# Splitting the first two experts' weights on GpSimd in the front of an attention and mixture-of-experts kernel

## The reference

```python
xn = _layernorm(x)
out = x + attention(xn) + ffn(xn)

# attention: 16 heads of 8, causal mask
q, k, v = split(xn @ in_proj.T)
p = softmax(q @ k.T / sqrt(8) + mask)
attention = (p @ v) @ out_proj.T

# ffn: one shared expert and 7 routed ones, the best 2 for each token
expert(h, g, u, d) = (silu(h @ g.T) * (h @ u.T)) @ d.T      # 128 -> 352 -> 128
probs = softmax(xn @ wr.T + rb); the two largest, scaled to sum 1
ffn = shared(xn) + sum over the two chosen experts of weight * expert(xn)
```

## Time and profile before

| what | us |
|---|---|
| time, median of 3 runs without a profile | 467.42 (467.25 to 471.32) |
| the profiled execution (its span, the one time that its page has) | 485.8 |
| TensorE busy in the profiled execution | 439.9 (91%) |
| GpSimd busy | 302.7 (62%) |
| granted TensorE clock, mean | 0.987 |

### The profile page before, as it was taken

One profiled execution on the slowest core, in us unless ns is written; L12 is line 12 of the kernel. 1 busy time (PEld: TensorE's weight loads), 2 busy tenths in 40 slices (PEclk: granted clock), 3 DMA queues, 4 the chain that ended last, 5 costly groups with the idle time before them and its releaser, 6 DMA issues.

```text
span 485.8 us, 12527 instructions
## 1 busy us (share of the span) xinstructions
PE 439.9 (91%) x3983; PEld 329.3 (68%) x3987; DVE 359.8 (74%) x804; ACT 312.8 (64%) x709; POOL 302.7 (62%) x439
## 2 busy tenths in 40 slices
PE   8888897988998989999889999998999899979995
PEld 4666565665666666666555688786877788868884
DVE  6885997987878877778774387585765777566987
ACT  2756676775867677767677676565565766555552
POOL 1326887997887888887888500755547487845300
PEclk9999999998999999999999999999999999989998
DMA  8776798999875555666356337787777767821762
GB/s 233 229 240 233 230 329 294 295 332 331 266 232 153 156 164 174 173 177 168 119 165 255 90 84 214 242 290 225 225 234 247 239 195 258 299 60 35 245 204 65
DMA packets 60415, 102.00 MB, mean 210 GB/s; under 512 B 11045, under 2 KB 29226, under 8 KB 59328
## 3 DMA queue, kind: packets, MB, share of 16 engines
q1 hardware_dynamic: 55872, 92.74, 61.2%
q0 software_dynamic: 4480, 8.47, 5.2%
HBM read 62.49 MB, written 39.46 MB: 210 GB/s over the span
## 4 chain that ended last, share of the span: by engine, by line
PE 62%; ACT 7%; POOL 6%; issue 5%; DVE 4%; SPq 4%; DMA 2%; another core or an unknown queue 2%; DVEq 0%; ACTq 0%; POOLq 0%
PE ps L850 11%; PE ps L848 11%; PE ps L849 11%; PE ps L917 6%; PE ps L978 6%; PE ps L925 4%; ACT sb_work L706 4%; POOL sb_work L620 3%; POOL xs L596 2%; PE ps L998 2%; DMA sb_ring<-qk 2%; PE ps L1143 2%; PE ps L981 2%; SPq L471 2%
## 5 line engine op out<-in xcount | busy, mean ns | idle before, releaser
L1343 DVE TENSOR_REDUCE sb_blockmax<-ps 128x6 f32<-128x768 f32 x128 | 121.5, 956 | 37.2 <-PE ps L925 32.4
L706 ACT ACTIVATE sb_work<-ps 128x768 f32<-128x768 f32 x128 | 104.7, 818 | 64.7 <-PE ps L913 63.5
L648 POOL DMA_INDIRECT ys<-sb_v_all,sb_xn_all x76 | 81.3, 1069 | 72.3 <-DVE sb_v_all L1464 52.6
L620 POOL TENSOR_SCALAR_AFFINE_SELECT sb_work<-sb_work 128x512 f32<-128x512 f32 x128 | 82.2, 646 | 27.6 <-ACT sb_work L706 25.5
L849 PE MATMUL ps<-sb_ring,sb_wb 128*128 128x512 f32 (+1 forms) x231 | 83.6, 362 | 0.0
L1443 DVE TENSOR_TENSOR sb_v_all<-ps,sb_v_all 128x512 f32<-128x512 f32 (+1 forms) x93 | 57.5, 618 | 24.4 <-ACT sb_v_all L796 10.6
L596 POOL DMA_INDIRECT xs<-sb_xn_all,sb_posu x64 | 62.9, 983 | 10.6 <-issue 10.6
L917 PE MATMUL ps<-sb_ring 32*128 32x256 f32 x256 | 49.5, 377 | 20.7 <-ACT sb_work L706 10.1
L796 ACT ACTIVATE sb_v_all<-ps 128x512 f32<-128x512 f32 (+1 forms) x93 | 49.7, 534 | 10.5 <-PE ps L850 5.4
L917 PEld LDWEIGHTS ps<-sb_ring 32*128 32x128 f32 x256 | 25.6, 183 | 44.9 <-issue 38.4
L848 PE MATMUL ps<-sb_ring,sb_wb 128*128 128x512 f32 (+1 forms) x138 | 51.6, 374 | 3.3 <-issue 1.8
(11 more groups left out here) (168 smaller groups left out, 1089.0 us busy)
## 6 DMA issues: line engine op xcount, KB each, us to landing
sb_wb<-wd SPq DMA_DIRECT2D x75, 384.0 KB
sb_ring<-qk SPq DMA_DIRECT2D x64, 256.0 KB
wd<-sb_wb SPq DMA_DIRECT2D x8, 1152.0 KB, 5.9
xs<-sb_o_all SPq DMA_DIRECT2D x19, 260.0 KB, 4.2
qk<-sb_ring SPq DMA_DIRECT2D x32, 128.0 KB
sb_work<-ys SPq DMA_DIRECT2D x16, 256.0 KB, 3.2
sb_xn_all<-xs SPq DMA_DIRECT2D x15, 260.0 KB
sb_o_all<-w SPq DMA_DIRECT2D x8, 384.0 KB, 3.9
```

The costliest lines, as they stand in the source:

```text
L620: pool.affine_select(out=o, in_=o, compare_op=ALU.is_ge, fill=0.0, base=0, pattern=[[0, 4], [1, 128]], channel_multiplier=-1)\
L648: pool.indirect_dma_start(out=ys_d, out_offset=bass.IndirectOffsetOnAxis(ap=row, axis=0), in_=yst[i % NYS][:, EMB * j:EMB * j + EMB], in_o ...
L706: act.activation(part.rearrange("p (k h q) -> p h k q", h=2, q=128), ps[:, 4:6, 0:HEAD].rearrange("p h (k q) -> p h k q", q=128), ACT.Exp, ...
L1343: dve.tensor_reduce(blockmax[:, a:b + 1, 0:3], ps[:, a:b + 1, 0:HEAD].rearrange("p h (k c) -> p h k c", c=128), AX.X, ALU.max).then_inc(s[ ...
```

## The change

A constant `AHEAD = 2` says how many experts are split in the front.

- GpSimd: in the front's loop over its six norm pairs, each pair is followed by one block: expert 0's three blocks behind `f = 5, 7, 9`, expert 1's behind `f = 11, 13, 15`. The memsets of `v_sb` and `ones_b`, which stood ahead of `split_block` in the file, now follow that loop. In the steps, the block at `n` is that of the expert two further on, and the last is at `n = 16` in place of 22.
- SP: the loads of experts 0 and 1 move from `n = -4` and `n = -1` to the place ahead of the constant tile's four DMAs. At `n = -4` and `n = -1` SP now loads experts 2 and 3, which wait for the splits of 0 and 1, and stores 0 and 1. The later loads stand at `n = 2, 5, 8, 11`, the stores at `n = 2, 5, ..., 17`.
- TensorE, VectorE and ScalarE have the same instructions in the same order.

```diff
+AHEAD = 2
...
+            for e in range(AHEAD):
+                load_expert(e)
             sp.wait_ge(s["kzero"], 1)
             sp.wait_ge(s["kone"], 1)
             for b in range(4):
...
-                if (n + 4) % 3 == 0 and 0 <= (n + 4) // 3 < EXPERTS:
-                    load_expert((n + 4) // 3)
-                if (n - 2) % 3 == 0 and 0 <= (n - 2) // 3 < EXPERTS:
-                    store_expert((n - 2) // 3)
+                if (n + 4) % 3 == 0 and AHEAD <= (n + 4) // 3 + AHEAD < EXPERTS:
+                    load_expert((n + 4) // 3 + AHEAD)
+                if (n - 2) % 3 == 0 and 0 <= (n - 2) // 3 + AHEAD < EXPERTS:
+                    store_expert((n - 2) // 3 + AHEAD)
...
-            for f in range(5, NB, 2):
+            for i, f in enumerate(range(5, NB, 2)):
                 pool.wait_ge(s["rs"], f // 2 + 1)
                 for t in (2 * f, 2 * f + 1):
                     last = pool.tensor_scalar(...)
                 last.then_inc(s["xp"], 1)
+                split_block(i // MT, i % MT)
...
-                if 0 <= n + 1 < MT * EXPERTS:
-                    split_block((n + 1) // MT, (n + 1) % MT)
+                if 0 <= n + 1 < MT * (EXPERTS - AHEAD):
+                    split_block((n + 1) // MT + AHEAD, (n + 1) % MT)
```

More of the change, by code:

```diff
@@ L593, in split_block @@
                 pool.wait_ge(s["wsp"], e + 1)
+            for i, f in enumerate(range(5, NB, 2)):
+                pool.wait_ge(s["rs"], f // 2 + 1)
+                for t in (2 * f, 2 * f + 1):
+                    last = pool.tensor_scalar(xn_all[:, t, 0:EMB], x_sb[:, t, :], mv[:, t, 0:1], rstd[:, t:t + 1],
+                                              ALU.subtract, ALU.mult)
+                last.then_inc(s["xp"], 1)
+                split_block(i // MT, i % MT)
+            for k, buf in enumerate(v_sb):
+                pool.memset(buf, 0.0).then_inc(s["vz"], 1)
+                pool.wait_ge(s["vz"], k + 1)
+                pool.memset(buf[:, :, :, HD:HD + 1], 1.0).then_inc(s["v1"], 1)
+            pool.memset(ones_b[:, :], 1.0).then_inc(s["onesb"], 1)
             def send(k, t):
```

## The result

The changed kernel took 476.91 us (median of 4 runs, 471.80 to 479.24) against 467.34 us before (466.43 to 471.32). The ratio is 1.0162, 95% interval 1.0111 to 1.0214: 1.6% slower, outside the range of 463.0 to 471.8. An execution over 1.5% above the shortest of its kernel (here that of 479.24) counts as slow and is in no ratio, so a ratio can differ from the quotient of the medians (here 1.0205). The profiled execution is one of 478.70 us, with a span of 477.0.

The account below looks back on a forecast made before the run. TensorE was taken as busy for 91% of the span, with VectorE pacing 27 to 39 us of the front. The terms +1.9 + 0 + 1.0 - 2.3 - 0.6 came to 0.0 us: 467.5 us, range 463.0 to 471.8.

Parts of the forecast that it names:

- The loads ahead of the constant tile: Front: ten DMAs on SP delay writes and first read-back, so the front ends 1.9 us later (0.6 to 3.5).
- The blocks behind the norms: Front: GpSimd's split blocks fit its gaps, hidden behind VectorE's statistics, at no cost; about 1 us if expert 0 loads late.
- SP behind GpSimd: Steps 3 to 9: SP's queue waits for GpSimd's blocks, +1.0 us (0 to 2.9); as slower rival 472.6 us, chance 0.18.
- The later experts sooner: Steps 17 to 25: without those loads, splits and stores, 2.3 plus 0.6 us gained, 2.9 together (0 to 5.5).
- The rivals: DMA relief 462.5 us (0.18), SP's queue 472.6 (0.18), VectorE's routing pacing steps 17 to 22 469.7 (0.09), port lock 469.6 (0.05).
- The ports: Front rival: VectorE's five shifts each wait for a GpSimd subtraction on shared ports, +2.2 us, 469.6 us, chance 0.05.

Follow-up runs that it names:

- before_again: The kernel before, unchanged, run for a second profiled execution: 467.76 us, with a span of 466.0 us.
- third_buffer: The changed kernel with a buffer of its own for sequence 2's query and key pair: 474.87 us, ratio 1.0153 to the kernel before.
- fill: The changed kernel with 22 unused matmuls on constant data in TensorE's two waits: 472.08 us, ratio 1.0094 to the kernel before.
- one_ahead: The changed kernel with expert 1's load moved behind the first three read-backs: 469.24 us, ratio 1.0044 to the kernel before.
- pool_loads: The changed kernel with the first two experts' ten load DMAs on GpSimd's queue, before its first norms: 468.07 us, ratio 1.0030.
- tile_first: The changed kernel with only expert 0's load early, behind the constant tile, and four zero fills moved to later steps: 469.44 us, ratio 1.0042.

## Why the prediction was wrong

The profiled executions of before_again and of the changed kernel give the account: front +11.6 us, steps 0 to 2 -0.4, steps 3 to 8 +0.9, steps 9 to 16 +0.1, steps 17 to 25 -1.2. That is +11.0, and the spans differ by 11.0 (477.0 less 466.0); the medians, by 9.6. The forecast had +1.9, 0, +1.0, 0 and -2.9. No term of the forecast had the -0.4: in steps 0 to 2 the kernel before has a granted clock of 0.84 and the changed one 1.00, as their windows show; why was not found.

- *The loads ahead of the constant tile: +1.9, wrong.* This is the step that failed. Its rows were right at first: the constant tile was forecast at 14.95 and went at 15.02; sequence 0's writes at 17.5 and went at 17.65. Two things were missing behind that. The writes were followed only to the read-back, and not to the buffer that they free: `qk_h[0]`, for which ScalarE waited 1.95 us and TensorE 2.70 in place of 0.89. And "the front ends 1.9 us later" took every later instruction at its old duration. With waits of 2 to 3 us in it TensorE fell to 1.2 GHz and became the bound in VectorE's place. third_buffer shows that taking the first wait away is not enough, fill that the clock is some 8 of the 11.6 us. The read-back itself was also later than forecast (25.27, not 23.85), because SP was held up inside the writes (2.08 us for two; the upper bound of 3.5 had allowed for such a hold-up), and step -3 began at 29.00, not 27.3.
- *The blocks behind the norms: 0, right.* In one_ahead they are all there and step 0 begins at 44.24 us against 44.11.
- *SP behind GpSimd: +1.0, right by number, not by reason.* 22.93 less 22.03 is 0.9. But that holds for a front 11.6 us late; with the front in time steps 3 to 8 lose 3.6 us (one_ahead) or 3.3 (pool_loads), above the upper bound of 2.9, which was worked out for just that case, and steps 3 to 16 lose 2.7 or 2.0, within it.
- *The later experts sooner: -2.9, mis-sized.* The steps do run at 3.40 us each (20.42 / 6). But the 22.9 us to which this was compared came from one execution that was disturbed in that place; the typical loss there is 21.05 less 20.42, 0.6 us, and 1.2 with steps 23 to 25. The prediction saw that its profiled execution was 18.4 us over the median and carried the difference over "one to one". The reason why that execution was slow was not found; it was slower in every stretch behind 129 us as well (steps 26 to 62 took 127.53 us, 124.05 in the second profile, and what lies behind step 63's first exponential 217.9 and 204.1).
- *The rivals.* None of them came as described. SP behind GpSimd is real, at 2.0 to 2.7 us over steps 3 to 16, but was mostly hidden. The ports are real and cost nothing (below); the prediction's row against them was no test, since its shift and its norm began together.

The four runs of the changed kernel spread widely, and by their granted clock: 471.80 us at 0.992, 475.13 at 0.982, 478.70 at 0.966, 479.24 at 0.968. That fits a low clock of different length in each; only the profiled one has a trace.

## What to carry to other kernels

Whoever moves DMAs ahead of others in a queue has to follow every semaphore of those that are pushed back: the consumer of the data, and also whoever refills the buffer that they read, a wait that leaves no row while it has slack. Where TensorE gains a wait, price the stretch behind it at 1.2 GHz too, and see which engine is the bound then. And take the durations to be saved from an execution whose span agrees with the median, or from two.

## What the runs showed of the hardware

- The low clock outlasted the waits. In the changed kernel TensorE was busy for 11.52 of 12 and 12.78 of 13 us at a granted clock of 0.50 before it rose to 1.00 at 52 us. In tile_first it was low for about 10 us (0.99 from 24 to 29, 0.50 from 29 to 39, 0.99 from 39 to 48.7). What decides between the two lengths stays open.
- In tile_first the clock fell behind a wait of 0.83 us at step -3, 2 us after one of 0.89 that the kernel before has too; in one_ahead, which has the 0.89 and no wait at step -3, it stayed at 1.00. That the 0.83 by itself decided it is not shown.
- VectorE's shift ran 0.47 us instead of 0.18 where it met a subtraction of GpSimd, and ended within 0.03 us of that subtraction (GpSimd's three began at 20.63 and took 1.29):

```profile
21.48 0.47 DVE L1194 SCALAR_TENSOR_TENSOR sb_shifts<-sb_mv,sb_rstd 128x4 f32<-128x4 f32 x1
```

  The rule of the Trainium skill that the prediction weighed ("SBUF — State Buffer", section "SBUF: two separate sides") agrees with the trace here, for a subtraction of two tensors. In all the kernels run, the shifts that began inside a subtraction took 0.21 to 0.49 us and the others 0.16 to 0.19. Beside a norm the shift kept its 0.18 us in the changed kernel too (at 14.56), as in the earlier trace rows. That is not against the rule, which asks which of the two starts first: there both begin within 0.01 us of each other, and no run has a shift that begins inside a running norm. So the prediction's "the trace does not agree" said more than its row. Two lengthened shifts in one_ahead (0.47 and 0.37 us) had no effect on its step 0.
